# Local attention in 32-row blocks: score tiles of 32 queries by 4 heads, probabilities turned on VectorE, value tiles of 32 by 64, rotation on GpSimd

## What is computed

```python
def l2norm(t):
    return t / jnp.clip(jnp.linalg.norm(t, axis=-1, keepdims=True), 1e-12)

def _layer(x, wqkv, qs, ksc, wo, lg, lb, w1, b1, w2, b2):
    h = shift_token(x)                  # second half of the features comes from the token before
    q, k, v = jnp.split(h @ wqkv, 3, axis=-1)      # 8 heads of 64 each
    q = l2norm(q) * qs
    k = l2norm(k) * ksc
    q, k = rotary_xpos(q, k)            # a*cos*scale + rotate_half(a)*sin*scale
    o = local_attention(q, k, v)        # key j is seen by query i where i-64 <= j <= i
    x = x + o @ wo
    ...                                 # layer norm, gelu network
```

## Time and profile before

| | |
|---|---|
| median of 3 runs | 1703.03 us (1700.28 to 1703.07) |
| profiled execution, its own time | 1697.82 us |
| its span, first to last instruction | 1695.8 us |
| mean granted clock of PE | 0.938 of full speed |
| busy: PE / DVE / ACT / POOL | 87% / 77% / 61% / 34% |

### The profile page before, as it was taken

The page is one execution under the profiler, slowest core; times in us unless marked ns, Lnnn a source line. Parts: engine busy times, 40 slices in busy tenths (PEclk is TensorE's granted clock), DMA queues, the critical chain, the costliest instruction groups (busy, mean ns, idle before and its releaser), DMA issues. The chain is left out here.

```text
span 1695.8 us, 45799 instructions
## 1 busy us (share of the span) xinstructions
PE 1479.6 (87%) x17522; PEld 801.5 (47%) x17532; DVE 1301.7 (77%) x3513; ACT 1029.6 (61%) x2227; POOL 568.6 (34%) x618
## 2 busy tenths in 40 slices
PE   5876999997669999999999799987899787999975
PEld 3632344433424555555555566655566552333333
DVE  5636788884978788778878699766999567898848
ACT  2331666665846666666655598833898522777764
POOL 0306656620010000000002598524999104343200
PEclk9995999998979999999999999998999995999997
DMA  5124433401010000000000000010100003222100
GB/s 173 31 36 129 96 88 84 79 28 51 1 40 3 9 3 9 9 9 3 29 3 3 8 1 0 1 49 17 34 0 0 15 6 83 49 50 42 31 2 25
DMA packets 61570, 56.41 MB, mean 33 GB/s; under 512 B 9866, under 2 KB 53054, under 8 KB 61254
## 3 DMA queue, kind: packets, MB, share of 16 engines
q1 hardware_dynamic: 60518, 53.42, 13.0%
q10 hardware_dynamic: 864, 0.39, 0.1%
HBM read 30.59 MB, written 1.05 MB: 19 GB/s over the span
## 5 line engine op out<-in xcount | busy, mean ns | idle before, releaser
L1953 ACT ACTIVATE probs_l2x<-probs_l2x,nmax_l2x 128x512 f32<-128x512 f32 x256 | 182.7, 715 | 154.8 <-DVE nmax_l2x L1823 154.5
L1823 DVE CUSTOM_DVE_ANT_0 probs_l2x<-s_ps_l2x,mask_b_l2x 128x512 f32<-128x512 f32 x248 | 161.1, 687 | 86.9 <-PE s_ps_l2x L2032 85.2
L1087 DVE CUSTOM_DVE_ANT_0 junk_l1x<-s_ps_l1x,mask_b_l1x 128x512 bf16<-128x512 f32 x256 | 166.2, 687 | 43.3 <-PE s_ps_l1x L1292 41.3
L1090 DVE TENSOR_REDUCE nmax_l3x<-s_ps_l3x 128x1 f32<-128x512 f32 x256 | 163.9, 684 | 32.5 <-PE s_ps_l3x L1292 30.7
L1149 ACT ACTIVATE pT_l1x<-st_ps_l1x 128x1024 f32<-128x1024 f32 x128 | 131.2, 1025 | 70.5 <-PE st_ps_l1x L1277 70.5
L1835 DVE STREAM_TRANSPOSE pT_l2x<-probs_l2x 128x512 f32<-128x512 f32 x256 | 166.4, 688 | 0.0
L2032 PE MATMUL s_ps_l2x<-kT_l2x_first,q_l2x 64*32 64x512 f32 x1984 | 137.7, 612 | 11.0 <-DVE nmax_l2x L1823 10.1
L2048 PE MATMUL pv_ps_l2x<-pT_l2x,v_l2x_first 32*64 32x256 f32 x4096 | 124.0, 383 | 3.5 <-issue 3.5
L2643 POOL TENSOR_TENSOR rn_l2a_first<-ssc_l2a_first,consts 128x16 f32<-128x16 f32 x28 | 109.1, 3895 | 20.2 <-DVE ssc_l2a_first L2670 20.0
L2813 ACT ACTIVATE probs_l2a<-minus_s_l2a,nmax_l2a 128x128 f32<-128x128 f32 (+1 forms) x256 | 106.1, 424 | 9.5 <-DVE nmax_l2a L2718 9.5
L2048 PEld LDWEIGHTS pv_ps_l2x<-pT_l2x,v_l2x_first 32*64 32x64 f32 x4096 | 91.2, 132 | 39.7 <-issue 15.2
(11 more groups left out here) (536 smaller groups left out, 3598.7 us busy)
## 6 DMA issues: line engine op xcount, KB each, us to landing
mask_i_l1x<-in_mask SPq DMA_DIRECT2D x8, 512.0 KB, 4.9
maskT_i_l1x<-in_mask_t SPq DMA_DIRECT2D x8, 512.0 KB, 5.2
kT_l1x_first<-parts_l1x_first SPq DMA_DIRECT2D x60, 64.0 KB
kT_l3x_first<-parts_l3x_first SPq DMA_DIRECT2D x60, 64.0 KB
q_l1x<-parts_l1x_first SPq DMA_DIRECT2D x90, 32.0 KB
q_l3x<-parts_l3x_first SPq DMA_DIRECT2D x90, 32.0 KB
ctxT_l0x<-in_ctxT SPq DMA_DIRECT2D x9, 256.0 KB, 3.2
rows_l0x<-in_ctx SPq DMA_DIRECT2D x9, 256.0 KB, 4.2
```

What stands on the lines that cost most here:

```text
L1087: dve.tensor_tensor_reduce(out=junk[w][:], in0=s_ps[w][:], in1=mask_b[b % 2][:, j, :], scale=-1.0, scalar=3e38, op0=ALU.add, op1=ALU.min, ...
L1090: dve.tensor_reduce(to, s_ps[w][:], AX.X, ALU.max, negate=True).then_inc(m.s_drained[w].sem, 1)
L1823: dve.tensor_tensor_reduce(out=probs[n % 4][:], in0=score_bank(b, s, w), in1=mask_b[b % 2][:], scale=-1.0, scalar=3e38, op0=ALU.add, op1=A ...
L1953: act.activation(probs[n % 4][:], probs[n % 4][:], ACT.Exp, bias=nmax[:, b % 2, n:n + 1], scale=-1.0, accum_out=sums[:, r, w, qb:qb + 1]). ...
```

## The change

Scores. The tile of scores is now 32 queries by up to 96 keys (the block of 32 itself and the two before it), and the four heads 2c+w of one w stand in the four 32-partition quarters. A bank holds four such query blocks; two banks, w = 0 and 1, make half of the queries of all 8 heads. `scores(b, u, h)` fills both for the half h; `maxima` and `exponentials` then take each of the 16 units a batch in one operation, in place in `probs`. The mask shrinks to one 32x96 pattern.

Turning. The exponentials' sums are inverted on DVE, the probabilities are multiplied by them on DVE, and a DVE transpose turns each 32x32 block into `pT`. PE's transposes, the copies out of PSUM, the bf16 splitting of the inverses, their spreading and the scaling of o are gone.

Outputs. For each block of 32 keys, 4x2 tiles of 32 keys by 64 dimensions are multiplied with up to three query blocks, all into one PSUM tile, which one ACT operation copies. The product with `wo` follows in the next batch's turn and for the last batch behind the loop.

Rotation and powers. `own_part` moves from DVE to POOL. The power -0.5 moves from POOL to ACT as Ln and Exp, with one table set loaded ahead.

Values and ring. Values are projected 32 tokens at a time and stand first in the order; the ring has two banks instead of four.

```diff
@@ FirstLocal
+    def project_values(self, pe, n, out, tokens):
+
+        half = S // BLK // TPB
+        for e in range(half):
+            kb = half * n + e
+            for c in range(P // BLK):
+                ins = pe.matmul(out[BLK * c:BLK * (c + 1), e * P:(e + 1) * P], tokens[:, BLK * kb:BLK * (kb + 1)],
+                                self.wqkv[:, 2 * 512 + c * P:2 * 512 + (c + 1) * P], start=True, stop=True)
+        return ins
@@ local_attention
-    DEEP, RING = 2, 4
+    NQ = S // BLK
+    HALF = NQ // 2
+    BACK = 2
+    SPAN = (BACK + 1) * BLK
+    RING = 2
...
+    order = [V, V + 1, TURN, TURN + 1, QK, QK + 1, TURN + 2, TURN + 3, QK + 2, QK + 3]
@@ gpsimd
+                def own_part(b, j, at):
+                    pool.wait_ge(*ring.full(*(at if not (isinstance(b, int) and b == 1) else (lambda f: prepared(0, f)))(TURN + 2 * j + 1)))
+                    pool.tensor_tensor(own[:, j], qk[:, j], ta[:, :, j, :].unsqueeze(2).to_broadcast([P, 2, NH, HD]), ALU.mult)\
+                        .then_inc(m.rotated.sem, 1)
@@ vector
+                def turn_probs(b, h):
+
+                    dve.wait_ge(*m.probs_ready.after(unit(b, h, 1, HALF)))
+                    dve.reciprocal(inv[:, h, :], sums[:, h].rearrange("p w n -> p (w n)")).then_inc(m.sums_inverted.sem, 1)
+                    dve.wait_ge(*m.sums_inverted.after(2 * b + h + 1))
+                    units = probs[h][:].rearrange("p w n k -> p (w n) k")
+                    dve.tensor_tensor(units, units, inv[:, h, :].unsqueeze(2).to_broadcast([P, 2 * HALF, SPAN]), ALU.mult)\
+                        .then_inc(m.probs_scaled.sem, 1)
...
+                    for w in range(2):
+                        dve.transpose(pT[:, w, HALF * h:HALF * (h + 1), 0:SPAN], probs[h][:, w]).then_inc(m.turned.sem, 1)
...
+                    maxima(b, 1)
+                    if left >= 1:
+                        normalise(b + 1, 0)
+                    turn_probs(b, 0)
+                    if left >= 1:
+                        sum_squares(b + 1, 1)
+                    add_outputs(b, m.y_padded[:, bass.ds(TPB * (2 * i + u), TPB), :])
+                    turn_probs(b, 1)
+                    if left >= 1:
+                        normalise(b + 1, 1)
+                        maxima(b + 1, 0)
+                    if left >= 2:
+                        sum_squares(b + 2, 0)
@@ scalar
+                def power(b, j):
+
+                    of = slice(j * 2 * NH, (j + 1) * 2 * NH)
+                    act.wait_ge(*m.squares_ready.after(TPB * b + j + 1))
+                    act.activation(logs[:, of], ssc[:, of], ACT.Ln).then_inc(m.logs_ready.sem, 1)
+                    act.wait_ge(*m.logs_ready.after(TPB * b + j + 1))
+                    act.activation(rn[:, of], logs[:, of], ACT.Exp, scale=-0.5).then_inc(m.powers_ready.sem, 1)
...
+                act.preload_act_table_set("natural_log_exp_and_others")
...
+                    exponentials(b, 1, 0)
+                    empty_bank(V)
+                    empty_bank(V + 1)
+                    exponentials(b, 1, 1)
+                    empty_bank(TURN)
+                    empty_bank(TURN + 1)
+                    empty_bank(QK)
+                    empty_bank(QK + 1)
+                    if left >= 1:
+                        power(b + 1, 1)
...
+                    act.wait_ge(*m.pv_done.after(b + 1))
+                    act.activation(o[:], pv_ps[:, :, 0:S], ACT.Copy).then_inc(m.pv_copied.sem, 1)
+                    empty_bank(TURN + 2)
+                    empty_bank(TURN + 3)
+                    if left >= 1:
+                        exponentials(b + 1, 0, 0)
+                    empty_bank(QK + 2)
+                    empty_bank(QK + 3)
+                    if left >= 1:
+                        exponentials(b + 1, 0, 1)
+                    if left >= 2:
+                        power(b + 2, 0)
@@ tensor
+                def scores(b, u, h):
+
+                    pe.sem_inc(m.passed.sem, 1)
+                    for w in range(2):
+                        rows = slice(HD * w, HD * (w + 1))
+                        for n in range(HALF):
+                            qb, of = HALF * h + n, cols(h, n)
+                            for c in range(NG):
+                                ins = pe.matmul(s_ps[w][BLK * c:BLK * (c + 1), n * SPAN + of.start:n * SPAN + of.stop],
+                                                q[u][rows, c, BLK * qb:BLK * (qb + 1)], kT[u][rows, c, keys(h, n)], start=True, stop=True)
...
+                    pe.wait_ge(*m.max_ready.after(unit(b, 0, 1, HALF)))
+                    scores(b, u, 1)
+                    output_products(b)
+                    for f in (V, V + 1, TURN, TURN + 1, QK, QK + 1):
+                        take(f)
...
+                        scores(b + 1, 1 - u, 0)
+                    outputs(b, u)
+                    for f in (TURN + 2, TURN + 3, QK + 2, QK + 3):
+                        take(f)
+                    for f in (TURN + 2, TURN + 3):
                         pe.wait_ge(*ring.empty(*turn(i, u, f)))
```

More of the change, by code:

```diff
@@ L2804, in _, with exponentials @@
+                def exponentials(b, h, w):
+                    for n in range(HALF):
+                        act.wait_ge(*m.max_ready.after(unit(b, h, w, n + 1)))
+                        act.activation(probs[h][:, w, n, cols(h, n)], probs[h][:, w, n, cols(h, n)], ACT.Exp, bias=nmax[:, h, w, n:n + 1],
+                                       scale=-1.0, accum_out=sums[:, h, w, n:n + 1]).then_inc(m.probs_ready.sem, 1)
+                act.preload_act_table_set("natural_log_exp_and_others")
                 for b, f in AHEAD_OF_LOOP:
@@ L2820, in _ @@
                                    ACT.Copy).then_inc(ring.drains(*shifted(w)[1:]), 1)
-                act.wait_ge(*m.zeroed.after(10))
-                exponentials(0, 0, 0)
+                act.wait_ge(*m.zeroed.after(4))
+                for w in range(2):
+                    exponentials(0, 0, w)
+                power(1, 0)
                 for f in range(TURNS):
@@ L2923, in fill @@
-                    ins.then_inc(ring.fills(*at[1:]), 1)
-                def scores(i, u, g):
-                    halves = [(s_ps[hh], slice(HD * hh, HD * (hh + 1))) for hh in range(2)]
-                    for out, rows in halves:
-                        pe.matmul(out[:, 0:P], q[u][rows, g, 0:P], kT[u][rows, g, 0:P], start=True, stop=True)
-                    for out, rows in halves:
-                        pe.matmul(out[:, TILES[1]], q[u][rows, g, P:S], kT[u][rows, g, 64:S], start=True, stop=True).then_inc(m.scores_ready.sem, 1)
+                        ins = local.project_values(pe, f - V, bank, hs[1 - u])
@@ new lines, in outputs @@
+                def outputs(b, u):
+                    pe.wait_ge(*m.turned.after(4 * b + 4))
+                    pe.wait_ge(*m.out_added.after(b + 1))
+                    pe.sem_inc(m.passed.sem, 1)
+                    for kb in key_order:
+                        n = min(BACK + 1, NQ - kb)
+                        for c in range(NG):
+                            for w in range(2):
+                                blocks = pT[BLK * c:BLK * (c + 1), w].rearrange("p a t -> p (a t)")
+                                lo = kb * P + BACK * BLK
+                                of = blocks[:, lo:lo + (BACK + 1) * (P - BLK)].rearrange("p (s t) -> p s t", t=P - BLK)[:, 0:n, 0:BLK]
+                                to = pv_ps[HD * w:HD * (w + 1), c, BLK * kb:BLK * (kb + n)].rearrange("p (s t) -> p s t", t=BLK)
+                                ins = pe.matmul(to, v[u][BLK * c:BLK * (c + 1), kb, HD * w:HD * (w + 1)], of, start=(kb == 0), stop=(kb == key_order[-1]))
+                    ins.then_inc(m.pv_done.sem, 1)
@@ L2933, in _, with output_products @@
+                def output_products(b):
+                    pe.wait_ge(*m.pv_copied.after(b))
+                    for j in range(TPB):
+                        for g in range(NG):
+                            ins = pe.matmul(out_ps[:, j * D:(j + 1) * D], o[:, g, j * P:(j + 1) * P], wo[:, g, :], start=(g == 0), stop=(g == NG - 1))
+                    ins.then_inc(m.out_filled.sem, 1)
                 for b, f in AHEAD_OF_LOOP:
@@ L3517, in shape_constants @@
     c["last"] = last
-    for name, per in (("spread4", 4), ("spread2", 2)):
+    for name, per in (("spread4", 4),):
         groups = HEADS // per
```

342 lines of the change are left out of this document (91 added, 251 removed).

## The result

The changed kernel takes 1738.05 us (median of 4 runs, 1731.23 to 1741.60), the kernel before 1703.05 (1700.28 to 1704.71) beside it: a ratio of 1.0206, 95% interval 1.0182 to 1.0229. It is slower by 2%, where the prediction had 1681 and at most 1706. The profiled execution is the shortest of the four: 1731.2, with a span of 1729.4.

A forecast was written before the change was run, and what follows sets the result against it. Four nearly full engines bound the local attentions, and after the change their order. Each stage: 15.8 + 6x18.6 + 16.5 + 12.1 = 156.0 for 166.9; twice, plus 0.5 for constants, 1703.0 - 22.3, about 1681; range 1655 to 1706.

The forecast's parts named there:

- What bounds the kernel before: Local attentions: DVE, PE, POOL and ACT all close to full in batches of 18.5 or 19.7 us; all four need relief.
- the operations' costs: Work per batch of the local attentions: DVE 18.2 to 15.3 us, ACT 17.1 to 15.6, PE about 19 to 12.
- rival D: ACT's Ln and Exp each reload their table despite the preload: 22 us a batch, 1722; chance 0.04.
- Where it waits: Walk of one batch through the engines' order, with DVE and POOL excluding each other: 18.6 us a batch.
- rival B: POOL's big product stands before DVE twice a batch, 1.6 us each beyond 0.6: 21.8 a batch, 1719; chance 0.16.
- C: Half clock on PE's two projections and turns before the next scores: 20.7 us in a batch hit, 1706; chance 0.08.
- PE's small tiles: PE's score and output matmuls bound by columns: scores 0.64 and 0.48 us, outputs 1.1 a batch.
- rival E: Starts, 27 ns each, bound PE's small matmuls: outputs 3.4 us instead of 1.1, 19.7 a batch, 1694; chance 0.04.
- The edges: Each local stage's ends: first step about 15.8 us after the start, seventh batch 16.5, eighth 12.1.
- The second chain: ACT's copies, exponentials, square and power, which the next normalise awaits, then 11.0 us of DVE: 18.3 a batch.
- rival A: POOL's products fall beside DVE's reductions, maxima and turns, so meetings are light: 17.2 us a batch, 1663; chance 0.25.

The follow-up runs named there:

- pieces: Changed kernel with POOL's own-table product of 128x1024 written as four of 128x256: 1699.2 us, ratio 0.9978 to the kernel before.
- whole, full clock: Changed kernel, POOL's product uncut, with extra unused matmuls in PE's waits to hold the clock: 1744.4 us, ratio 1.0244 to the kernel before.
- kernels with early scores: Changed kernel, product in four, next scores ahead of two projections: 1716.1 us; also with ACT's powers and exponentials ahead of its projection copies: 1675.1.

## Why the prediction was wrong

- What bounds the kernel before, and the operations' costs: right. DVE's products of 128x768 take 0.96 (0.95), its turns 0.56 each (0.48), POOL's product 2.38 when nothing holds it up (2.4), Ln and Exp 0.42 (0.5); each stage has one table load of 1.28, so rival D is out. Two of its sums are off by their own terms: DVE's comes to 15.5 and not 15.3, ACT's to 15.0 and not 15.6 (15.1 to 15.4 measured). Neither carries the 18.6, which is walked and not summed.
- The step that failed stands under "Where it waits": the long hold was counted as 0.6 a meeting, and rival B set aside because "after the four small ones DVE has usually asked first". The runs showed 1.9 and 2.0 a hold, two in eight batches and 20 in all. In 8 of them POOL's product had begun before DVE's addition asked. In the other 12 DVE had asked first and still lost: its normalising is two instructions with a semaphore between them, and POOL's product, asked for during the addition, gets the lock in that gap. B's price was right, 21.8 a batch for 22.1 measured at full clock, though it placed one of the two holds before the scaling of the probabilities and both fall on the normalising. B as a whole stood at 1719, and the kernel took 1738.
- B and C were weighed as alternatives, and they came together: DVE held, PE idle, clock down, turns and projections ahead of the next scores longer. 18.2 (pieces, full clock), 22.1 (whole, full clock), 23.8 (whole, half clock over the projections) show the two steps, 3.9 and 1.7; a range made of one rival at a time could not hold their sum. That the holds bring the fall fits the eight batches but isn't shown: with four pieces the clock falls too, in every other batch of the first stage, and once over these projections (3.72, in a batch of 21.4).
- PE's small tiles: mis-sized, without much weight. At full clock 64 score matmuls take 1.26 and 1.10 (0.64 and 0.48 forecast from columns), 128 output matmuls 1.74 (1.1): on average 17 to 20 and 13.6 ns each. Columns don't bound them, and neither does the 27 ns of rival E; the floor of 25 ns that the Trainium skill gives ("TensorE: Matmul & The Clock Gate", Wait — 56ns, not 53.3ns?) is not seen between instructions on different parts of the array.
- The edges: the start had 18.4 and 17.8 for 15.8. The scores stand there behind turns of h, which wait 2.27 for ACT, and in the first stage they meet half clock themselves (2.17); the last batch had 15.0 for 12.1, which is half clock over its outputs and last product.
- The second chain, ACT's order, was in the prediction as 18.3 a batch. The kernels with early scores show it as the bound (20.6), and gone (17.1). No step of the prediction led to this 17.1, since it took the order as it was; rival A's 17.2 is near it by luck, for it came from lighter meetings with POOL.

What stays open: why the clock falls in some batches of the four pieces and not in others, and so how much of the 7 us that the pieces win beside DVE's own waits is the clock's; no run kept one and changed the other. The same holds for why PE's loop was loaded again in the first stage only.

## What to carry to other kernels

Before work is moved to GpSimd, look at the length of its single instruction and not at the sum: here VectorE lost nearly all of it at each meeting, and pairs of dependent VectorE operations with a semaphore between them invite it. Cut the instruction into pieces as short as the wait that can be borne (here up to 0.6 us); GpSimd pays for it, here 2.8 for 2.4 a product. When four engines are relieved at once, what is left is the order, so walk each engine's queue for what stands ahead of the operation that another one waits for, and price a stall of PE together with the fall of its clock, not as two rivals. Work put into a wait to hold the clock up is safe only where the wait stays longer than the work.

## What the runs showed of the hardware

A POOL product of 128x1024 (2.38 us) and four of 128x256 (2.78 to 2.80 together) do the same work; beside DVE's two-operand work the four delay it by up to 0.6 an operation, the one by up to 2.05. Score matmuls of 64x32 tiles come 17 to 20 ns apart on average, output matmuls of 32x64 tiles 13.6, at full clock. Fourteen bf16 matmuls of 256 columns in a wait of PE, outside the loop, kept the outputs behind it at 1.74 for 2.71. With 88 of them in a loop of two batches its instructions were loaded again in the first stage (21 packets for 3), and in the batch shown PE waited 2.59 and 2.29 us without a named releaser before and inside a burst; in the second stage the same loop had 4 packets, and its five batches after the first took 19.8 to 20.1.
